# Seven small tables instead of six, and a TensorE order by unit

## The reference

```python
e = jnp.stack([tbl_f[ids[:, f]] for f in range(32)], axis=1)      # [2048, 32, 256]
dots = jnp.einsum('bnd,bmd->bnm', e, e)
z = dots[:, iu, ju]                                               # upper triangle, 496
h = jnp.concatenate([z, dense_ctx], axis=1)                       # 512
h = jnp.maximum(h @ W_top1 + b_top1, 0.0)                         # 512
h = jnp.maximum(h @ W_top2 + b_top2, 0.0)                         # 256
y = h @ W_top3                                                    # 1
```

## Time and profile before

| | us |
|---|---|
| timed runs, median of 3 | 566.03 |
| lowest, highest | 565.94, 626.95 |
| span of the profiled execution | 890.7 |

### The profile page before, as it was taken

One profiled execution on the slowest core, in us unless ns is written; L12 is line 12 of the kernel. 1 busy time (PEld: TensorE's weight loads), 2 busy tenths in 40 slices (PEclk: granted clock), 3 DMA queues, 4 the chain that ended last, 5 costly groups with the idle time before them and its releaser, 6 DMA issues.

```text
span 890.7 us, 24184 instructions
## 1 busy us (share of the span) xinstructions
PE 601.0 (67%) x11019; PEld 524.1 (59%) x11019; DVE 225.9 (25%) x578; ACT 204.6 (23%) x369; POOL 398.0 (45%) x426
## 2 busy tenths in 40 slices
PE   3557668486684867748577584875848668486687
PEld 2456557375572756737467474765737657375586
DVE  3444313123130231402223032231312313123122
ACT  4252303103030030401313022130210303103042
POOL 7563625526255361543715347262462625526220
PEclk9688969698796987969789697896969969698799
DMA  9962312313122141321313224131231312313110
GB/s 220 243 204 68 99 42 77 94 44 102 43 78 83 50 107 38 83 73 56 108 37 87 63 57 118 32 96 49 70 105 39 101 41 76 88 41 90 43 38 2
DMA packets 37459, 70.97 MB, mean 80 GB/s; under 512 B 10382, under 2 KB 23438, under 8 KB 37358
## 3 DMA queue, kind: packets, MB, share of 16 engines
q0 software_dynamic: 20112, 54.95, 22.1%
q1 hardware_dynamic: 17246, 14.48, 7.0%
HBM read 69.39 MB, written 0.01 MB: 78 GB/s over the span
## 4 chain that ended last, share of the span: by engine, by line
PE 42%; another core or an unknown queue 30%; issue 13%; ACT 12%; DMA 1%; DVE 1%; POOL 1%; ACTq 0%; DVEq 0%
PE look_ps L338 18%; PE quad_ps L358 12%; PE top_ps L420 6%; ACT turned L501 4%; ACT turned L483 3%; PE turn_ps L322 3%; PE quad_ps L322 2%; ACT area L550 2%; ACT ahead L490 1%; DMA rows<-in_tbl,row_ids 1%; PE quad_ps L377 1%; POOL rows L295 1%; PE top_ps L407 1%; ACT products L506 0%
## 5 line engine op out<-in xcount | busy, mean ns | idle before, releaser
L295 POOL DMA_INDIRECT rows<-in_tbl,row_ids x419 | 397.2, 948 | 458.1 <-PE turn_ps L322 184.1
L338 PE MATMUL look_ps<-one_hot,small 125*128 125x256 f32 (+1 forms) x1536 | 251.9, 303 | 104.7 <-issue 92.8
L338 PEld LDWEIGHTS look_ps<-one_hot,small 125*128 125x128 f32 x1536 | 214.0, 202 | 116.6 <-issue 112.3
L358 PE MATMUL quad_ps<-turned 128*32 128x31 f32 x7680 | 140.0, 204 | 121.8 <-issue 121.5
L358 PEld LDWEIGHTS quad_ps<-turned 128*32 128x32 f32 x7680 | 108.8, 115 | 166.9 <-issue 153.3
L674 DVE TENSOR_SCALAR one_hot<-ids_across,sub_row 125x256 fp32r<-125x256 int32 (+1 forms) x384 | 112.0, 364 | 145.8 <-PE look_ps L338 126.6
L322 PE MATMUL turn_ps<-ident,rows 128*128 128x128 f32 x424 | 64.5, 282 | 28.5 <-issue 14.7
L655 DVE TENSOR_TENSOR top_ps<-top_ps,b_sb 128x256 f32<-128x256 f32 x15 | 6.5, 433 | 299.8 <-PE top_ps L420 299.8
L490 ACT ACTIVATE ahead<-look_ps 128x512 f32<-128x512 f32 (+1 forms) x48 | 28.3, 590 | 232.5 <-PE look_ps L338 219.1
L407 PE MATMUL top_ps<-area,w_sb 128*128 128x128 f32 x488 | 61.9, 276 | 19.5 <-issue 18.8
L550 ACT ACTIVATE area<-top_ps,b_sb 128x128 f32<-128x128 f32 x61 | 17.5, 368 | 227.5 <-remote 225.2
(11 more groups left out here) (50 smaller groups left out, 169.9 us busy)
## 6 DMA issues: line engine op xcount, KB each, us to landing
rows<-in_tbl,row_ids POOLq DMA_INDIRECT x419
ids_across<-in_small_ids SPq DMA_DIRECT2D x45, 128.0 KB
landed<-in_tbl SPq DMA_DIRECT2D x6, 896.0 KB
w_sb<-in_W_top SPq DMA_DIRECT2D x4, 256.0 KB
landed<-in_tbl SPq DMA_DIRECT2D x6, 104.0 KB
w_sb<-in_W_top SPq DMA_DIRECT2D x1, 512.0 KB
area<-in_dense_ctx SPq DMA_DIRECT2D x16, 8.0 KB
row_ids<-in_ids SPq DMA_DIRECT2D x1, 240.0 KB
```

The lines of the kernel that those rows point to most:

```text
L295: pool.indirect_dma_start(out=rows[:, n % PLACES, j, :], out_offset=None, in_=tables[f], in_offset=bass.IndirectOffsetOnAxis(ap=row_ids[:, ...
L338: last = pe.matmul(look_ps[:, c * width:(c + 1) * width], small[:, f, r, part, c * P:(c + 1) * P], one_hot[n % 2][:, r, 0:width], start=(r ...
L358: last = pe.matmul(gram_ps[q * FIELDS:(q + 1) * FIELDS, g // BANK_GROUPS, at:at + COLS], turned[:, c, s, :], turned[:, c, s, 0:COLS], star ...
```

## The change

- Field 14 joins the small tables: four even ones (fields 2, 4, 5, 6) and three odd ones (8, 9, 14). A later tile gathers 25 fields (12 pairs and one single), tile 0 has 28.
- `split_high` is one copy, and `split_low` one subtraction with both inputs in SBUF; each table is a tensor of its own.
- Lookups are made in the tile whose rows they give first. ScalarE writes the first tile's half of a result straight into `turned`, the second half into `ahead`, which halves per table; `place` moves the latter alone. Lookups have two banks, turnings three.
- TensorE takes a tile in 13 slots: a unit is turned, then comes that slot's share of the lookup products (`SLOT_SHARES`), and the features, layer 1 and layer 2 of the tile before in slots 2, 5 to 8 and 12 (10 in the last tile). Then come all gram products in one run.
- SyncE loads the numbers of lookup n+3 where n is used; `load_ids(5)` still follows the weights.
- SBUF set aside for dynamic transfers is 4096 bytes a partition.

```diff
-EVEN_FIELDS = [2, 4, 5]
-ODD_FIELDS = [6, 8, 9]
+EVEN_FIELDS = [2, 4, 5, 6]
+ODD_FIELDS = [8, 9, 14]
...
-    ACT_UNITS = [0, 1, 2, 6, 8, 10, 12]
-    RING = 4
+    ACT_UNITS = [0, 2, 4, 6, 8, 10, 12]
+    RING = 3
+    LOOKS = 2
     LOOK_AFTER = [2, 5, 8, 11]
-    SPLIT_AFTER = [0, 2, 5, 8]
-    EARLY_AFTER = [3, 4, 5, 6]
-    TURN_FEATURES_AFTER = 6
-    PARTS = 8
+    HIGH_AFTER = [0, 2, 5, 7, 8, 10, 12]
+    LOW_AFTER = [0, 2, 5, 7, 9, 11, 13]
+    FEATURES_SLOT = 2
+    LAYER1_SLOTS = [5, 6, 7, 8]
+    LAYER2_SLOT = 12
+    LAST_LAYER2_SLOT = 10
+    SLOT_SHARES = [11, 11, 7, 11, 11, 3, 3, 3, 3, 11, 11, 11, 0]
...
+    for t in range(TILES):
+        FIRST[t] = len(LOOKUPS)
+        LOOKUPS += [(f, t, min(2, TILES - t)) for f in (range(EVENS) if t % 2 == 0 else range(EVENS, SMALL))]
...
-        ahead = sbuf("ahead", [P, SMALL, CHUNKS, 2 * P])
+        ahead = sbuf("ahead", [P, SMALL, CHUNKS, P])
...
-            load_ids(5)
             for t in range(TILES):
-                if t + 2 in FIRST:
-                    for n in range(FIRST[t + 1], FIRST[t + 2]):
-                        load_ids(n)
-                if t + 1 < TILES:
-                    load_dense(t + 1)
+                for n in range(FIRST[t], FIRST[t + 1]):
+                    if t > 0 and n == FIRST[t + 1] - 1:
+                        load_dense(t)
+                    if n >= 2 and n + 3 < len(LOOKUPS):
+                        load_ids(n + 3)
...
+            def all_in_place(t):
+                pe.wait_ge(act_kept, n_act_kept(BEGIN[t + 1] - 1))
+                pe.wait_ge(dve_kept, n_dve_kept(BEGIN[t + 1] - 1))
+                pe.wait_ge(look_placed, FIRST[t + 1])
...
+            gram(0)
+            for t in range(1, TILES):
+                for i in range(BEGIN[t + 1] - BEGIN[t]):
+                    turn(BEGIN[t] + i)
+                    look_in_slot(t, i)
+                    if i == FEATURES_SLOT:
+                        turn_features(t - 1)
+                    if i in LAYER1_SLOTS:
+                        layer1(t - 1, LAYER1_SLOTS.index(i))
+                    if i == (LAST_LAYER2_SLOT if t == TILES - 1 else LAYER2_SLOT):
                         layer2(t - 1)
+                if t < TILES - 1:
+                    gram(t)
+                else:
+                    last_gram()
...
             def keep_looked_up(n):
...
+                both = look_ps[n % LOOKS][:, 0:CHUNKS * tiles * P].rearrange("p (c t s) -> p t c s", c=CHUNKS, t=tiles)
+                act.activation(turned[:, :, :, f], both[:, 0, :, :], ACT.Copy).then_inc(look_placed, 1)
+                if tiles == 2:
+                    act.activation(ahead[:, f, :, :], both[:, 1, :, :], ACT.Copy).then_inc(look_kept, 1)
...
+                act.activation(small[i][:, :, 0, :], landed[i][:, :, 1, :], ACT.Copy).then_inc(high_ready, 1)
...
+                dve.wait_ge(high_ready, i + 1)
+                dve.tensor_tensor(small[i][:, :, 1, :], landed[i][:, :, 1, :], small[i][:, :, 0, :],
+                                  ALU.subtract).then_inc(low_parts, 1)
...
             for i in range(BEGIN[1]):
                 if i not in ACT_UNITS:
                     keep_turned(i)
-                if i in SPLIT_AFTER:
-                    split_low(SPLIT_AFTER.index(i))
-                if i in LOOK_AFTER[:2]:
+                if i in LOW_AFTER:
+                    split_low(LOW_AFTER.index(i))
+                if i in LOOK_AFTER:
                     make_one_hot(LOOK_AFTER.index(i) + 2)
-            make_one_hot(EVENS + 1)
...
-    nc = bacc.Bacc("TRN2", target_bir_lowering=False, num_devices=1)
+    nc = bacc.Bacc("TRN2", target_bir_lowering=False, num_devices=1, dynamic_dma_scratch_size=4096)
```

More of the change, by code:

```diff
@@ L87, in dlrm_tower @@
     LAST_GROUPS = GROUPS // LAST_BANKS
-    AT_ONCE = 2
-    STEPS = SUB // AT_ONCE
     IDS_RING = 3
-    OUTS = 4 * CHUNKS
     LOOKUPS, FIRST = [], {}
[L98 to L106, removed]
+    for t in range(TILES):
+        FIRST[t] = len(LOOKUPS)
+        LOOKUPS += [(f, t, min(2, TILES - t)) for f in (range(EVENS) if t % 2 == 0 else range(EVENS, SMALL))]
     FIRST[TILES] = len(LOOKUPS)
     PRODUCTS = CHUNKS * SUB * 2
+    SLOT_ENDS = [sum(SLOT_SHARES[:i + 1]) for i in range(len(SLOT_SHARES))]
     ctx = ExitStack()
@@ L126, in dlrm_tower @@
         one_hot = [sbuf(f"one_hot{i}", [SP, SUB, 2 * P], fp32r) for i in range(2)]
-        with nc.sbuf_tensor("landed", [SP, SMALL, SUB, 2, D], fp32) as landed:
-            pass
-        small = sbuf("small", [SP, SMALL, SUB, 2, D], fp32r)
+        small, landed = [], []
+        for f in range(SMALL):
+            with nc.sbuf_tensor(f"landed{f}", [SP, SUB, 2, D], fp32) as table_landed:
+                landed.append(table_landed)
+            small.append(sbuf(f"small{f}", [SP, SUB, 2, D], fp32r))
         rows = sbuf("rows", [P, PLACES, 2, D])
         turned = sbuf("turned", [P, CHUNKS, P, FIELDS])
-        ahead = sbuf("ahead", [P, SMALL, CHUNKS, 2 * P])
+        ahead = sbuf("ahead", [P, SMALL, CHUNKS, P])
         products = sbuf("products", [P, COLS * (ZROW + 1)])
@@ L146, in dlrm_tower @@
         gram_ps = quad_ps[:, 0:2, :]
-        turn_ps = [psum(f"turn_ps{i}", [P, 512]) for i in range(RING - 2)] + [quad_ps[:, b, :] for b in (2, 3)]
-        look_ps = psum("look_ps", [P, 512])
+        turn_ps = [psum(f"turn_ps{i}", [P, 512]) for i in range(RING - 1)] + [quad_ps[:, 2, :]]
+        look_ps = [psum("look_ps", [P, 512]), quad_ps[:, 3, :]]
         top_ps = psum("top_ps", [P, KC * P])
@@ L229, in n_gathered, with n_kept, lookups_done, done_in_slot @@
             return 16 * sum(len(UNITS[m][1]) for m in range(n % PLACES, n + 1, PLACES))
+        def n_kept(n):
+            return sum(tiles == 2 for _, _, tiles in LOOKUPS[:n])
+        def lookups_done(t, products):
+            return [n for n in range(FIRST[t], FIRST[t + 1]) if (n + 1 - FIRST[t]) * PRODUCTS <= products]
+        def done_in_slot(t, i):
+            made = (FIRST[t + 1] - FIRST[t]) * PRODUCTS
+            ends = [made * end // SLOT_ENDS[-1] for end in [0] + SLOT_ENDS]
+            return [n for n in lookups_done(t, ends[i + 1]) if n not in lookups_done(t, ends[i])]
         def n_ids(n):
@@ L342, in look_up, with gram @@
                     last.then_inc(looked_up, 1)
[L344 to L347, removed]
-                    pe.wait_ge(placed, 2 * t + 1)
-                    if t > 0:
-                        pe.wait_ge(unfolded, t)
-                if t == 0 and portion == PARTS // 2:
-                    pe.wait_ge(low_parts, SMALL * STEPS)
-                for g in range(portion * GPP, (portion + 1) * GPP):
+            def all_in_place(t):
+                pe.wait_ge(act_kept, n_act_kept(BEGIN[t + 1] - 1))
+                pe.wait_ge(dve_kept, n_dve_kept(BEGIN[t + 1] - 1))
+                pe.wait_ge(look_placed, FIRST[t + 1])
+                if t > 0:
+                    pe.wait_ge(placed, t)
+                    pe.wait_ge(unfolded, t)
+            def gram(t):
+                all_in_place(t)
+                for g in range(GROUPS):
                     at = g % BANK_GROUPS * COLS
@@ L360, in gram, with last_gram @@
                                              start=(c == 0), stop=(c == CHUNKS - 1))
[L361 to L371 removed]
+                last.then_inc(gram_done, 1)
+            def last_gram():
+                all_in_place(TILES - 1)
+                for g in range(GROUPS):
                     at = g % LAST_GROUPS * WIDE
```

161 lines of the change are left out of this document (51 added, 110 removed).

## The result

| | us |
|---|---|
| before, median of 4 runs | 565.99 |
| after, median of 4 runs (683.56 to 685.86) | 685.08 |
| ratio, 95% interval | 1.2136, 1.2095 to 1.2178 |
| forecast, range | 561, 542 to 583 |

The change made the kernel slower by 21%, far outside the range. The ratio is of the fast runs; one run of the kernel before took 626.95 us. From the page of the changed kernel: the span, busy time, the granted clock by slices, the queue of instructions, and the gram records with their idle time (busy, mean ns | idle before).

What follows compares the result with a forecast made beforehand. The prediction took GpSimd's gather issue to bound the kernel before, and TensorE the changed one: 74.6 + 14 x 30.8 + 31.7 for the last tile + 13.3 = 550.8, plus 10.5 around the span, 561 us; range 542 to 583.

Steps and rivals of the forecast that it cites:

- last tile and end: Closing terms of TensorE's sum: the last tile at 31.7 us, then 13.3 us to the end of the span.
- around the span: Time outside the profiled span: 10.5 us between the 555.5 us sum and the median, added to every sum.
- gram products in one run 5.6: TensorE's 512 gram records a tile, priced as eight times 0.70 us, the nearest row, as the lower end.
- second rival: Gram run outruns its instruction packets: at most 3.7 us a tile, 52 us over 14 tiles, 613 us; chance 0.25.
- last variant: Two packets in store, so the run's first comes free and every second later one is late: 1.4 us a tile, 581 us.
- The start: Tile 0: lookup 5's numbers land at 62 us, gram(0) starts at 69, GpSimd restarts at 75, 14.8 us lost.
- first rival: No wait at the start for lookup 5's numbers; gram(0) starts at 55, 14 us earlier: 547 us; chance 0.25.
- The slots: TensorE's tile outside the gram run: turnings 5.4, lookups 13.7, layers 5.6, features 0.5 us.
- The scratch: 4 KB for dynamic transfers: nothing put, a gain excluded; at worst GpSimd would wait for landings.
- third rival: Whole gain, no start wait, GpSimd's chain alone: 541 us, chance 0.1; obstacle, two-SBUF-input subtractions shutting out GpSimd's reads, seven times 2.7 us.
- The end: Tile 14's layers ahead of the last turning: last turning to last gram record 8.6 us instead of 14.0, -5.4 us.
- own range: Range of the central 561 us forecast alone, without rivals: 554 to 569 us, chance 0.4.

Runs made afterwards that it cites:

- e2: Kernel before, with lookups, second layer and first turnings moved ahead of the gram parts so all 512 records stand in one run: 691.79 us, ratio 1.2264.
- e8: Kernel before, with its 8 gram parts of 64 records joined into 4 runs of 128 in a tile: 576.73 us, ratio 1.0257.
- e9: Kernel before, with its 8 gram parts of 64 records joined into 2 runs of 256 in a tile: 651.56 us, ratio 1.1588.
- e12: Changed kernel, with two useless wide products after every 64 gram records from tile 1 on, 14 in a tile: 744.60 us, ratio 1.3213.
- e6: Changed kernel, with gram records moving 62 columns in place of 31, as many instructions: 662.88 us, ratio 1.1752.
- e1: Changed kernel, gram run cut into 8 parts of 64 records, with next tile's lookup products between and second layer after the first: 648.03 us, ratio 1.1469.
- e0: Kernel before, unchanged, profiled a second time: span 563.7 us, 565.5 us timed.
- e5: Kernel before, with only the scratch for dynamic transfers set to 4 KB: 562.92 us, ratio 0.9980.
- e13: Kernel before, with both layers of tile 14 put ahead of the last turning in the last tile: 563.04 us, ratio 1.0008.
- e10: Changed kernel, gram run in 8 parts with lookup products between, waits covered, ids loaded earlier, third lookup's one-hot matrix made ahead of unfolding grams: 614.14 us, ratio 1.0883.

## Why the prediction was wrong

The forecast's sum and the trace of the changed kernel, term by term:

| term | forecast | measured | difference |
|---|---|---|---|
| gram(0) begins | 69.0 | 70.0 | +1.0 |
| run of tile 0 | 5.6 | 12.4 | +6.8 |
| 14 runs | 14 x 5.6 | 14 x 13.26 | +107.2 |
| 14 times the rest of a tile | 14 x 25.2 | 14 x 26.23 | +14.4 |
| last tile and end | 45.0 | 48.8 | +3.8 |
| around the span | 10.5 | 1.8 | -8.7 |
| sum | 561 | 685.9 | +124.5 |

**The step that failed** is "gram products in one run 5.6", eight times a part of 64: 114 of the 124 us. The prediction called this the lower end, and the row had been read beside 22 instructions of lookup that last 1.50 us; taken away from there, its price no longer held. In its place the runs show 13.26 us (12.4 in tile 0), with 5.5 us of it gaps in which TensorE waits for the next 256 instructions. The other 2.2 us over 5.6 are slower records: 128 take 1.93 us where the granted clock is 0.50, against 1.40 by the earlier trace rows, and some bursts have short hitches. e2, e8, e9 and e12 show that the run itself is at fault, e6 that its length does not come from TensorE's work, and the record of the packets that each gap ends just after one has landed.

**The second rival** had the mechanism, its place and its sign, "gaps of 'issue' inside the run, about one in 253 instructions", but not the size. It let the request cost as much again as the transfer, 2.3 us to a packet. The bursts follow each other in 3.5 to 4.0 us, with a transfer of the same 1.1 us; so what stands beside the transfer takes more than twice the transfer. A gap is 1.8 us in the mean (0.8 to 2.9), not 0.9. Its 52 us became 107 in the same 14 tiles, and it left out the clock behind the run. Of its last variant half held: the first 138 to 249 records of a run came free, but then every packet was late, not every second one. The Trainium skill ("Runtime: NRT & Kernel Launch", Instruction fetch mechanics) calls crossing a block of 256 instructions mostly hidden. Here it is nearly hidden where a block lasts 3.3 us (144 instructions in 1.85 us, e1) and not where it lasts 1.4 us (the run), and the measurement decides. A chance of 0.25 for this rival and a range that cut it at 583 were the errors of judgement: its size had no row, and the prediction bounded it by doubling the one figure that it had.

**What bounds the kernel before.** The prediction put GpSimd 2.0 us a tile above TensorE. By e0 GpSimd is the bound, with a gather each 1.25 us and no wait from 80 us on, but only 1.4 us a tile above TensorE. The remaining 10.5 us of its sum do not lie around the span (1.8 us do): in e0 the last gather ends at 532.7 us, not 526.2 (4.5 of these 6.5 us are a wait for tile 1's first turning), and from the last turning to the end pass 29.1 us, not 27.3. Here the disturbed profile misled: its stalls had to be taken out by hand, and the waits of GpSimd in it could not be told from those of a timed run.

**What was right.** The start: numbers at 62, measured 64.2, so that the first rival did not come true; gram(0) at 69, measured 70.0; GpSimd held by tile 1's first turning, until 83.7 and not 75 because the run was longer. The slots: 25.2 a tile forecast, 25.0 measured where the clock held (e6). The scratch (e5). 403 gathers at 1.25 us. The third rival's obstacle is in the trace: the gather beside each of the seven new subtractions takes 2.06 to 2.97 us, not 0.95. The Trainium skill ("SBUF — State Buffer", Who interferes with whom) says that a VectorE instruction with two SBUF inputs contends with a GpSimd instruction that reads SBUF, and the trace agrees. The forecast put nothing for this on GpSimd's chain. It is 12.5 us in all: the 46th gather begins at 71.8 us, not near 59. That cost nothing here only because the next gather had to wait until 83.7 us anyway.

```profile
15.37 2.94 POOL L298 DMA_INDIRECT rows<-in_tbl,row_ids  x1 [0.30 <-issue]
...
15.20 2.29 DVE L638 TENSOR_TENSOR small<-landed,small 125x2048 fp32r<-125x2048 f32 x1 [2.26 <-ACT small L547]
```

**The end** was right in the trace (9.0 us from the last turning to the last record, 8.6 forecast) but is no gain of 5.4 us: e13 shows that the layers delay the turning that they are put ahead of, by 3.2 us.

**Would the change have paid without the gaps?** With the run at 5.6 and the rest at 25.0 its tile would take 30.6 us against 32.3, and with the other measured terms the sum is 70.0 + 15 x 5.6 + 14 x 25.0 + 48.8 + 1.8 = 555 us. This estimate lies in the forecast's own range, 554 to 569. No kernel here got there: filled with lookups (e10) the tile takes 35.2, 1.9 more than the unbroken prices in the stage and 2.7 more in the rest. Of the 1.9, 1.0 are still gaps of "issue"; of the 2.7, 1.2 are waits for ScalarE's copies. The filled stage is itself near the pace of the packets: its 1,152 instructions in 15.4 us are 256 in 3.4 us. That is shown for these arrangements, not for all.

## What to carry to other kernels

Price a long run of short instructions by the instructions, not by the work: here 256 of them per 3.5 to 4.0 us kept coming, and blocks of long products between short records were what had hidden this. A row's duration holds for the neighbours that it was measured beside; when an edit takes the neighbours away, the row is a lower end and the upper end needs a row of its own. And take a second profile where the first differs from the timed runs.

## What the chip showed that I had not expected

- 256 instructions reach TensorE per 3.45 to 4.02 us in a starved run, with gathers issued beside them or not, though their transfer takes 1.1 us. Some 1.2 us pass before the transfer and 1.4 us behind it; what happens in these was not tried.
- Twice the columns in the starved run made the kernel 22 us faster (685.1 to 662.9): in the run shown the granted clock stayed at 1.00 where it had fallen to 0.50.
- 13.4 us of useless products in a stage of 13.3 us lengthened it by 5.9.
